# Attention with a mixture of experts: probabilities kept whole in float32, and a float32 values product in two halves of the array's columns

## What is computed

```
qh = q.reshape(b, s, 4, 4, 64).transpose(0, 2, 3, 1, 4)     # q = layernorm(x)
kh = vh = ctx.reshape(b, s, 4, 64).transpose(0, 2, 1, 3)
scores = einsum('bghsd,bgtd->bghst', qh, kh) * 0.125
probs = softmax(scores)
out = einsum('bghst,bgtd->bghsd', probs, vh)
x = x + out.reshape(b, s, 1024) @ Wc.T + bc
x = x + experts(layernorm(x))          # router, top 8 of 32, gate/up/down
```

## Time and profile before

| | us |
|---|---|
| median of 3 runs | 9702.04 |
| lowest and highest | 9699.02, 9710.63 |
| profiled execution, its span | 9705.4 |

### The profile page before, as it was taken

The page is one execution under the profiler, slowest core; times in us unless marked ns, Lnnn a source line. Parts: engine busy times, 40 slices in busy tenths (PEclk is TensorE's granted clock), DMA queues, the critical chain, the costliest instruction groups (busy, mean ns, idle before and its releaser), DMA issues.

```text
span 9705.4 us, 172457 instructions
## 1 busy us (share of the span) xinstructions
PE 9157.1 (94%) x44592; PEld 7702.0 (79%) x44593; DVE 6503.2 (67%) x10304; ACT 4465.8 (46%) x7458; POOL 5282.3 (54%) x5081
## 2 busy tenths in 40 slices
PE   7898898898895999999999999999999999999999
PEld 5776777677774888888888888888888888888888
DVE  7888888888885566666655656666666566656565
ACT  6676666676673333333333333333333333333333
POOL 3444444444445566565655656555666555655564
PEclk8999999999997999999999999999999999999999
DMA  2111111111112555555544655555555455555554
GB/s 88 48 53 49 50 51 49 51 53 48 49 51 72 108 112 132 113 112 117 112 106 106 137 109 110 118 111 125 118 112 111 106 118 108 134 109 111 114 123 80
DMA packets 664527, 918.18 MB, mean 95 GB/s; under 512 B 338193, under 2 KB 477457, under 8 KB 663954
## 3 DMA queue, kind: packets, MB, share of 16 engines
q0 software_dynamic: 209920, 604.72, 29.2%
q1 hardware_dynamic: 454162, 308.44, 12.2%
HBM read 1064.79 MB, written 376.45 MB: 148 GB/s over the span
## 4 chain that ended last, share of the span: by engine, by line
PE 60%; DMA 3%; issue 3%; DVE 2%; ACT 1%; SPq 1%; POOL 0%; DVEq 0%; ACTq 0%; POOLq 0%
PE bank L1576 39%; PE bank L1599 21%; DMA gu_raw<-in_L_ffn_up_proj 3%; SPq L1311 1%; DVE gu_lo L1490 0%; ACT xT_hi L1403 0%; DVE xT L1479 0%; ACT gu_hi L1410 0%; DVE h L1502 0%; DVE d_lo L1495 0%; DVE h_lo L1507 0%; DVE h_hi L1505 0%; DVE xT_lo L1484 0%; POOL xg L1363 0%; DVEq L41 0%
## 5 line engine op out<-in xcount | busy, mean ns | idle before, releaser
L1363 POOL DMA_INDIRECT xg<-xn_rows,gather_row x2304 | 2766.7, 1201 | 2086.7 <-PE bank L1576 1310.6
L1576 PE MATMUL bank<-xT_hi,gu_hi 128*128 128x512 f32 (+2 forms) x6912 | 2553.4, 369 | 102.8 <-DVE xT_lo L1484 94.5
L1576 PE MATMUL bank<-xT_lo,gu_hi 128*128 128x512 f32 (+2 forms) x6912 | 2543.2, 368 | 0.0
L1576 PE MATMUL bank<-xT_hi,gu_lo 128*128 128x512 f32 (+2 forms) x6912 | 2543.1, 368 | 0.0
L1421 ACT ACTIVATE gated<-bank 128x512 f32<-128x512 f32 x432 | 258.2, 598 | 3030.0 <-PE bank L1576 2740.1
L1576 PEld LDWEIGHTS bank<-xT_hi,gu_hi 128*128 128x128 f32 x6912 | 1299.2, 188 | 278.6 <-issue 91.5
L1375 POOL DMA_INDIRECT out_rows<-rows_out,entry_now x576 | 1129.0, 1960 | 671.6 <-DVE rows_out L1514 322.5
L1576 PEld LDWEIGHTS bank<-xT_lo,gu_hi 128*128 128x128 f32 x6912 | 1299.7, 188 | 158.9
L1576 PEld LDWEIGHTS bank<-xT_hi,gu_lo 128*128 128x128 f32 x6912 | 1299.1, 188 | 158.9
L1502 DVE TENSOR_TENSOR h<-bank,gated 128x512 f32<-128x512 f32 x432 | 297.6, 689 | 1578.5 <-ACT gated L1421 1133.8
L1599 PE MATMUL bank<-d_hi,h_hi 128*128 128x512 f32 x3162 | 1257.3, 398 | 76.7 <-DVE h_lo L1507 76.7
(11 more groups left out here) (162 smaller groups left out, 14769.3 us busy)
## 6 DMA issues: line engine op xcount, KB each, us to landing
gu_raw<-in_L_ffn_gate_proj SPq DMA_DIRECT2D x576, 384.0 KB
gu_raw<-in_L_ffn_up_proj SPq DMA_DIRECT2D x576, 384.0 KB
d_raw<-in_L_ffn_down_proj SPq DMA_DIRECT2D x144, 1536.0 KB
xg<-xn_rows,gather_row POOLq DMA_INDIRECT x2304
x_t<-in_x SPq DMA_DIRECT2D x64, 512.0 KB, 4.4
inv_wide<-inverse_sums SPq DMA_DIRECT2D x512, 64.0 KB
out_rows<-x SPq DMA_DIRECT2D x64, 512.0 KB, 5.0
xn_rows<-xn SPq DMA_DIRECT2D x64, 512.0 KB
```

The source lines that it names most:

```text
L1363: pool.indirect_dma_start(out=xg[:, m, :], out_offset=None, in_=quarter_rows, in_offset=bass.IndirectOffsetOnAxis(ap=gather_row[:, m:m + 1 ...
L1576: last = nc.tensor.matmul(bank[:, 0:cols], w[:, c, n, j * P:(j + 1) * P], v[:, c, 0:cols], start=(c == 0 and w is gu_hi and v is xT_hi), s ...
```

## The change

The transposed probabilities are kept in one float32 tile pT instead of a hi and a lo part. For three heads of a group ScalarE copies them, for head 1 of each group VectorE does (`DVE_HEAD`), both `copy_probs`; two semaphores, pt_by_act and pt_by_dve, count them, and `by_act` and `by_dve` give the counts. v is a float32 copy of the context with 64 columns. The values product has float32 operands: for each chunk two matmuls, r = 0 and 1, with the same stationary v; each takes the heads r and r + 2 as 256 moving columns and writes 64 partitions from 64 r on, the layout that the projection needs. Chunks 0 and 1 are issued in slots with h % 4 = 1 and chunks 2 and 3 where h % 4 = 3. o_low, o_sum and their steps are gone; VectorE multiplies the bank itself with the inverse sums, in the slots of the former sum.

The context is loaded twice, side by side, so that a float32 transpose gives the keys in both halves of the partitions. ScalarE writes the hi part from each half (`keys_hi`, two instructions of 64 partitions), VectorE the lo part of each half by a subtraction (`keys_lo`, two). `load_ctx` is eight DMAs. The diff, cut to its core (in the parts left out the old steps are removed from the lists of `tile` and the new ones put in their places, as the text says):

```diff
--- before.py
+++ after.py
...
 
             INVERT = {4 * g + 2: g for g in range(G)}
-            OUT_SUM = {0: (1, 2), 4: (1, 3), 8: (0, 0), 12: (0, 1)}
-            OUT_SPLIT = {h + 1: back_group for h, back_group in OUT_SUM.items()}
+            OUT_NORM = {0: (1, 2), 4: (1, 3), 8: (0, 0), 12: (0, 1)}
+            OUT_SPLIT = {h + 1: back_group for h, back_group in OUT_NORM.items()}
+            DVE_HEAD = 1
+            VALUE_CHUNKS = {1: (0, 1), 3: (2, 3)}
 
             PROJECT = {0: (1, 0, 1, 2), 1: (1, 0, 2, 3), 2: (1, 0, 3, 4), 3: (1, 0, 4, 5), 4: (1, 0, 5, 6), 7: (1, 0, 6, 8),
                        8: (1, 1, 0, 2), 9: (1, 1, 2, 3), 10: (1, 1, 3, 4), 11: (1, 1, 4, 5), 12: (1, 1, 5, 6), 13: (1, 1, 6, 7),
...
@@ -290,9 +297,13 @@
                     sp.dma_start(xn_dram[bass.ds(j * P, P), :], xn2[:, :]).then_inc(xn2_stored, 16)
 
                 def load_ctx(b):
-                    wait(sp, vlo_ready, G * b)
-                    sp.dma_start(ctx_sb[:, :, :], ctx_v[:, bass.ds(b, 1), :, :].rearrange("p b c d -> p (b c) d")
-                                 ).then_inc(ctx_loaded, 16)
+                    wait(sp, v_ready, G * b)
+                    wait(sp, kt_done, G * b)
+                    for c in range(TC):
+                        for twice in range(2):
+                            sp.dma_start(ctx_sb[:, c, :, twice, :],
+                                         ctx_v[:, bass.ds(b, 1), c, :].rearrange("p b (g d) -> p (b g) d", d=HEAD_DIM)
+                                         ).then_inc(ctx_loaded, 16)
 
                 def load_x(i, s):
                     wait(sp, x2_ready, 2 * (i - SC) + 2)
...
@@ -424,15 +424,13 @@
                         if h == NEXT_BIAS and t.next:
                             add_bias(t.i + 1, t.next_s)
                         if h in SCATTERS and t.back3:
-                            hold(pthi_copied, H * t.i + h + 1)
+                            hold(pt_by_act, by_act(t.i, h))
                             scatter(t.i - 3, (SCATTERS[h],))
 
                 factors1(0)
                 queries_lo(0)
                 add_bias(0, 0)
                 all_tiles(pool, tile)
-                for g in (G - 2, G - 1):
-                    normalise_out(LAST, g)
                 factors2(LAST - 1)
                 scatter(LAST - 2, (0, 1, 2))
...
@@ -462,15 +460,16 @@
                     act.activation(qT[s % 2][:, 4 * n:4 * n + 4, :], MISC[0][:, :].rearrange("p (h t) -> p h t", h=4),
                                    ACT.Copy).then_inc(qt_copied, 1)
 
-                def values_hi(b, g):
-                    act.wait_ge(ctx_loaded, 16 * b + 16)
+                def copy_values(b, g):
+                    act.wait_ge(ctx_loaded, 16 * 2 * TC * (b + 1))
                     wait(act, pv_done, G * (SC * b - 1) + g + 1)
-                    act.activation(v[:, :, g, 0, :], ctx_sb[:, :, g * HEAD_DIM:(g + 1) * HEAD_DIM], ACT.Copy
-                                   ).then_inc(vhi_ready, 1)
-
-                def copy_keys(b, g):
+                    act.activation(v[:, :, g, :], ctx_sb[:, :, g, 0, :], ACT.Copy).then_inc(v_ready, 1)
+
+                def keys_hi(b, g):
+
                     act.wait_ge(kt_done, G * b + g + 1)
-                    act.activation(kT[:, g, :], O_BANK[g % 2][:, :], ACT.Copy).then_inc(kt_copied, 1)
+                    act.activation(kT[0:HEAD_DIM, g, :], O_BANK[g % 2][0:HEAD_DIM, :], ACT.Copy).then_inc(khi_copied, 1)
+                    act.activation(kT_swapped[HEAD_DIM:P, g, :], O_BANK[g % 2][HEAD_DIM:P, :], ACT.Copy).then_inc(khi_copied, 1)
 
                 def exponent(i, h):
                     act.wait_ge(max_ready, H * i + h + 1)
...
@@ -480,19 +479,13 @@
                     act.activation(probs[h % 4][:, :], S_BANK[h % 2][:, :], ACT.Exp, bias=neg_max[:, h:h + 1],
                                    accum_out=row_sum[:, h:h + 1]).then_inc(exp_ready, 1)
 
-                def copy_probs_hi(i, h):
+                def copy_probs(i, h):
                     g, k = divmod(h, GROUP_HEADS)
                     act.wait_ge(pt_done, H * i + h + 1)
                     if k == 0:
                         wait(act, pv_done, G * i + g - 1)
-                    act.activation(pT_hi[g % 2][:, :, k, :], PT_BANK[h % 2][:, :].rearrange("p (c t) -> p c t", c=TC),
-                                   ACT.Copy).then_inc(pthi_copied, 1)
-
-                def copy_out_low(i, g):
-
-                    act.wait_ge(pv_done, G * i + g + 1)
-                    wait(act, osum_ready, 2 * (G * i + g))
-                    act.activation(o_low[:, :], O_BANK[g % 2][HEAD_DIM:P, :], ACT.Copy).then_inc(olow_copied, 1)
+                    act.activation(pT[g % 2][:, :, k, :], PT_BANK[h % 2][:, :].rearrange("p (c t) -> p c t", c=TC),
+                                   ACT.Copy).then_inc(pt_by_act, 1)
 
                 def split_out_hi(i, g):
                     act.wait_ge(onorm_ready, G * i + g + 1)
...
@@ -589,16 +579,13 @@
                         wait(dve, ln1_ready, 2 * i)
                     statistics(n, ln1_chain, 2 * i, bn1, mv1, x_t[s], stats1)
 
-                def values_lo(b, g):
-                    dve.wait_ge(vhi_ready, G * b + g + 1)
-                    dve.tensor_tensor(v[:, :, g, 1, :], ctx_sb[:, :, g * HEAD_DIM:(g + 1) * HEAD_DIM],
-                                      v[:, :, g, 0, :].bitcast(F32), ALU.subtract).then_inc(vlo_ready, 1)
-
-                def copy_keys_swapped(b, g, half):
-                    dve.wait_ge(kt_copied, G * b + g + 1)
-                    to, at = ((0, HEAD_DIM), (HEAD_DIM, 0))[half]
-                    dve.tensor_copy(kT_swapped[to:to + HEAD_DIM, g, :], O_BANK[g % 2][at:at + HEAD_DIM, :]
-                                    ).then_inc(kts_copied, 1)
+                def keys_lo(b, g, half):
+
+                    dve.wait_ge(khi_copied, 2 * (G * b + g) + half + 1)
+                    rows = slice(half * HEAD_DIM, (half + 1) * HEAD_DIM)
+                    lo, hi = (kT_swapped, kT) if half == 0 else (kT, kT_swapped)
+                    dve.tensor_tensor(lo[rows, g, :], O_BANK[g % 2][rows, :], hi[rows, g, :].bitcast(F32), ALU.subtract
+                                      ).then_inc(klo_copied, 1)
 
                 def maximum(i, h):
                     dve.wait_ge(scores_done, H * i + h + 1)
...
@@ -613,20 +600,21 @@
                     wait(dve, inverse_stored, 64 * (G * i + g - 1))
                     dve.transpose(inv_turned[g % 2][:, :], row_inv[:, :]).then_inc(inverse_turned, 1)
 
-                def copy_probs_lo(i, h):
+                def copy_probs(i, h):
                     g, k = divmod(h, GROUP_HEADS)
-                    dve.wait_ge(pthi_copied, H * i + h + 1)
-                    dve.tensor_tensor(pT_lo[g % 2][:, :, k, :], PT_BANK[h % 2][:, :].rearrange("p (c t) -> p c t", c=TC),
-                                      pT_hi[g % 2][:, :, k, :].bitcast(F32), ALU.subtract).then_inc(ptlo_copied, 1)
-
-                def sum_out(i, g):
-
-                    dve.wait_ge(olow_copied, G * i + g + 1)
-                    wait(dve, onorm_ready, G * i + g)
-                    for r in range(2):
-                        hi, low = (o.rearrange("p (a two t) -> p a two t", two=2, t=P)[:, :, r, :]
-                                   for o in (O_BANK[g % 2][0:HEAD_DIM, :], o_low[:, :]))
-                        dve.tensor_tensor(o_sum[HEAD_DIM * r:HEAD_DIM * (r + 1), :, :], hi, low, ALU.add).then_inc(osum_ready, 1)
+                    dve.wait_ge(pt_done, H * i + h + 1)
+                    wait(dve, pv_done, G * i + g - 1)
+                    dve.tensor_copy(pT[g % 2][:, :, k, :], PT_BANK[h % 2][:, :].rearrange("p (c t) -> p c t", c=TC)
+                                    ).then_inc(pt_by_dve, 1)
+
+                def normalise_out(i, g):
+
+                    n = G * i + g
+                    dve.wait_ge(pv_done, n + 1)
+                    dve.wait_ge(inverse_wide, 32 * n + 32)
+                    wait(dve, otlo_ready, n)
+                    dve.tensor_tensor(o_norm[:, :, :], O_BANK[g % 2][:, 0:2 * P].rearrange("p (a t) -> p a t", t=P),
+                                      inv_wide[g % 2][:, :, :], ALU.mult).then_inc(onorm_ready, 1)
 
                 def split_out_lo(i, g):
                     dve.wait_ge(othi_ready, G * i + g + 1)
...
@@ -795,12 +779,11 @@
 
                 def transpose_keys(b, g):
 
-                    pe.wait_ge(vlo_ready, G * b + g + 1)
-
-                    wait(pe, osum_ready, 2 * (G * (SC * b - 1) + g + 1))
+                    pe.wait_ge(ctx_loaded, 16 * 2 * TC * (b + 1))
+                    wait(pe, onorm_ready, G * (SC * b - 1) + g + 1)
                     for c in range(TC):
-                        last = nc.tensor.transpose(O_BANK[g % 2][:, c * P:(c + 1) * P].bitcast(F32R),
-                                                   v[:, c, g, :, :].rearrange("p two d -> p (two d)"), ident_r[:, :])
```

(40 more changed lines are left out.)

73 lines of the change are left out of this document (29 added, 44 removed).

## The result

The changed kernel takes 9435.3 us (median of 4 runs, 9434.6 to 9436.5); the kernel before 9700.5 beside it. The ratio is 0.9723, interval 0.971 to 0.9736: 2.8% faster, 265 us. The forecast was 9577 us, 124 us less than before, and the range ended at 9440.

A forecast was written before the change was run, and what follows sets the result against it. TensorE in order was taken as the bound. Per tile, waits and clock -4.8, value matmuls +1.8, array changes +0.8, keys +0.2 gave -2.0 us, x 64 = -128 us: 9577 us, range 9440 to 9900.

The forecast's parts named there:

- What bounds the kernel: Attention tiles: TensorE in order is the bound, with 37 us of work per tile and 9 lost to waits and clock.
- The choice that decided: Value matmuls on TensorE: whether the two halves run beside each other (+1.8 us per tile, taken) or one behind the other (+7.4).
- Rival 1: Value matmuls: the halves run one behind the other, +7.4 us per tile in place of +1.8; 9900 to 9935 us, chance 0.34.
- Rival 3: Value matmuls: a float32 record of 256 columns takes 0.115 us, so visits are no dearer; 9462 us, chance 0.08.
- Rival 2: Halves run beside each other, but each change of array mode pays 0.16 us, 2.6 per tile; 9690 us, chance 0.10.
- The price of the value matmuls: TensorE, per tile: +1.8 us for visits of five steps of 0.23 us each, plus +0.8 for the array changes.
- the changes of layout: TensorE between whole and halved array: 16 changes per tile at 0.05 us each, +0.8 us.
- the keys' 0.2: Four key transposes per tile become float32, 0.07 to 0.11 us each, +0.2 us per tile.
- The relief: TensorE's waits and clock, per tile: -4.8 us, from 3.0 value wait, 1.0 scores' wait and 0.8 clock.
- the bound that I had named and not taken: Waits and clock, per tile: -6.8 us if value wait, scores' wait and clock loss all went.
- The clock: TensorE's granted clock of 0.95 costs up to 2.3 us per tile; a third, 0.8 us, was taken as regained.
- The wait of VectorE's product for inv_wide: VectorE's product with the inverse sums: its DMA is issued 11.8 us ahead, so waiting for it costs nothing.

The follow-up runs named there:

- e15: Changed kernel with ScalarE copying the transposed probabilities of all 16 heads and VectorE none; 9429.7 us.
- e4: Changed kernel with both halves of the heads sent to the same 64 partitions as one accumulation, output not the reference's; 9807.2 us.
- e2: Changed kernel with one chunk of the values in every slot, so 16 visits per tile to the halved array in place of 8; 9586.1 us.
- e3: Changed kernel with the loops of a visit exchanged, both chunks of half 0 and then both of half 1; 9440.4 us.
- e12: Kernel before without the lo part, o_low and o_sum, value pairs in slots 1 and 3, VectorE multiplying the bank with the inverse sums; 9425.3 us.
- e1: Kernel before with only the value chunks moved, issued as pairs in slots 1 and 3; 9662.8 us.
- e8: Changed kernel with all four chunks of a group in one visit, in the slot with h % 4 = 1; 9447.7 us.
- e13: Changed kernel with one four-chunk visit per group (h % 4 = 1), xn2 transposes one slot later, router in slot 7, top exponent in slot 9; 9389.3 us.
- e7: Kernel before without VectorE's subtraction for pT_lo, the values product using pT_hi twice, output not the reference's; 9496.7 us.

## Why the prediction was wrong in size

*What bounds the kernel: right.* The count of 37 us of TensorE work and the changed kernel's 39.5 us without a gap differ by about 2.45. Two parts of this are measured, the steps and the changes of layout; the keys' 0.2 is the forecast's own figure (see e15).

*The choice that decided: right.* The halves run beside each other (e4). The Trainium skill (TensorEngine Tiling (Array Packing), "Key Properties") says so of tiles of the array, and the 0.216 us for a pair of records agrees. Rival 1 would have been e4's case: 9807 us where 9900 to 9935 were said. Rival 3 is out: a record takes 0.216 us, not 0.115. Its time, 9462 us, is all the same the nearest to the measured one, by luck: pairs of 0.216 us cost a visit what single records of 0.115 would. Rival 2 has its price, a visit costs 0.34 us (e2), 2.7 per tile, but not its outcome.

*The price of the value matmuls: nearly right in the sum, by luck, and wrong in both terms.* I took +1.8 for five steps and +0.8 for the changes of layout. Measured are four steps, 8 x (0.864 - 0.92) = -0.45, and +2.7. With the keys' 0.2 that is +2.45 where 2.8 was forecast; one error covered the other. The error of the first term is the order that I gave the records (and 0.23 us for a step of 0.216); e3 shows that the halves don't keep it. The error of the second is that I read from alternating transposes and matmuls, which share one layout, what a change of layout costs. The Trainium skill's sentence that a change of tiling mode drains the engine (TensorEngine Tiling (Array Packing), "Key Properties") was the better guide. It gives no price; rival 2, to which it points, took 2.6 us per tile from the records' tails, and the runs gave 2.7.

*The relief: nearly right in size, wrong in its cause.* At unchanged TensorE work it is 46.19 - 40.74 = 5.45 us per tile (e12), where I had 4.8. But I gave 3.0 of it to the later slots, and these alone give 0.9 (e1); the subtraction on VectorE gives 4.0 alone, slots another 0.4, and the sums another 1.1. "What hides the copies now is that slot, and if it were gone the 3.0 us would stay" is the sentence that fell; e2 has the first chunk in the old slot, and they did not come back.

*The step that failed* is the sum itself: "-4.8 + 1.8 + 0.8 + 0.2", which lays the added work in full on top of the waits that are left. "Late next are the router, the query transposes and the jump, which the edits don't touch" says that these waits stay. That was wrong twice. First, the edits do touch them: in e12, where nothing is added to TensorE, the router's loads wait 0.4 us in 16 tiles and the queries' 1.5 (10.2 and 13.6 before), so the lighter VectorE and ScalarE took these waits. Second, what waits were left took in part of the added work, as I read it because a TensorE that comes later finds its operand nearer to ready: from e12 to e15 xn2's wait for ScalarE falls from 22.0 to 15.9 us and the scores' from 20.4 to 11.1 (14.3 and 10.8 behind the exponents, 6.1 and 0.3 "issue"). Of 2.45 us added only 0.9 reached the tile (e12 against e15), 1.1 against the changed kernel itself. So relief 0.65 more and price 1.7 less than forecast make the 2.35 us per tile that were missing: 4.36 came, 2.0 were forecast. Seen from the waits, the 9.1 us of waits and slow clock per tile fell to 2.3, by 6.8, the bound that I had named and not taken. To a time under 9440 us I had left a chance of about 0.05.

*The clock* moved with this: 0.95 to 0.99 over 16 tiles, 1.00 in ordinary ones, where I gave a third of the loss back.

*Smaller ones.* The wait of VectorE's product for inv_wide "costs nothing" was wrong by little: 6.5 us in 16 tiles. Loads of VectorE and ScalarE came within 0.5 us of the forecast. Three readings are off by little, and no sum rests on them: VectorE was busy 82% of the attention and ScalarE 69%, not 83% and 68%, and the quiet head takes 2.07 us, not 2.06.

What stays open: why a visit costs 0.34 us; the rows show where it lies, not what makes it. That GpSimd lost its four products had no run of its own.

## What to carry to other kernels

Count the bound engine's work densely, and treat its waits as one pool: an edit that only moved an instruction handed most of its wait to others in order (e1: 0.9 of 3.0 us were gained), and work added to that engine was paid in full only where no wait was left (e2, e4, e15). So bound a sum of relief and added work from the side where they overlap, and don't add them. Where a layout change has a fixed price, as here (e2), merge visits and look at once at which instruction then arrives too early (e8, e13).

## What the runs showed of the hardware

- Two column halves of the array work off their matmuls independently: with all of one half ahead of the other in the program, the second half's matmuls still start beside the first's (e3, four steps of 0.216 us for eight records; sent to one half, they take eight, e4).
- A float32 matmul of 256 columns is two records of 0.216 us, 0.43 us in all (e4, eight records in eight steps).
- Going to the halved layout and back costs 0.34 us (e2), about 0.09 of it ahead of the first matmul of the half, 0.15 within the visit and 0.11 behind it.
- The granted clock was 1.00, the level of 2.4 GHz, in tiles in which TensorE had no gap, and 0.92 to 0.96 in the ordinary tiles of the kernel before, which had gaps. It was also 1.00 in e7's ordinary tile, with 1.7 us of gaps in 39.7 us; at what gaps it falls, no run here was made to show.
